# Normalising the attention probabilities on VectorE instead of GpSimd, in a two-layer cross-attention and RWKV kernel

## The reference

```python
attn = jnp.einsum('bkhd,bnhd->bhkn', q, kmat) / DH
attn = jnp.where(full_mask[:, None, None, :], attn, -jnp.inf)
attn = jax.nn.softmax(attn.astype(jnp.float32), axis=-1)      # the change is inside this line
attn_out = jnp.einsum('bhkn,bnhd->bkhd', attn, v) @ out_w + out_b + residual
out = gelu(rmsnorm(attn_out) @ mlp_w1 + mlp_b1) @ mlp_w2 + mlp_b2 + residual
# layer 1: layer norm, token shift, five mixed inputs (w, k, v, r, g), then per head
#   out_t = r_t (u k_t v_t + s);  s = k_t v_t + w_t s;  group norm, gate, Wo, layer norm, channel mixing
```

## Time and profile before

| | |
|---|---|
| time, median of 3 runs | 1182.81 us (1182.03 to 1183.99) |
| the profiled execution | 1185.69 us, of which the span of its instructions is 1183.9 us |
| mean granted TensorE clock | 0.935 of full speed |
| TensorE busy | 1031.7 us, 87% |
| VectorE busy | 814.1 us, 69% |
| ScalarE busy | 715.7 us, 60% |
| GpSimd busy | 467.4 us, 39% |
| the 128 normalisations (L956), on GpSimd | 134.7 us busy |

### The profile page before, as it was taken

One profiled execution on the slowest core, in us unless ns is written; L12 is line 12 of the kernel. 1 busy time (PEld: TensorE's weight loads), 2 busy tenths in 40 slices (PEclk: granted clock), 3 DMA queues, 4 the chain that ended last, 5 costly groups with the idle time before them and its releaser, 6 DMA issues.

```text
span 1183.9 us, 20422 instructions
## 1 busy us (share of the span) xinstructions
PE 1031.7 (87%) x6760; PEld 764.9 (65%) x6760; DVE 814.1 (69%) x1275; ACT 715.7 (60%) x2006; POOL 467.4 (39%) x391
## 2 busy tenths in 40 slices
PE   5878989898998989898998989999898999988744
PEld 3656667676766767666676767677676767666523
DVE  2347677686867688696767768686776868677562
ACT  4466574848666493956658394765749476674312
POOL 1124263453425354343535434342534524253240
PEclk9799989899998999999998989899898989989776
DMA  4405050321415041231505033151503215050310
GB/s 140 144 27 78 27 74 13 62 41 46 70 41 73 14 79 23 55 60 41 73 18 89 8 67 48 41 74 41 73 14 62 41 42 73 18 74 10 47 34 9
DMA packets 37127, 61.02 MB, mean 52 GB/s; under 512 B 10464, under 2 KB 13088, under 8 KB 36896
## 3 DMA queue, kind: packets, MB, share of 16 engines
q1 hardware_dynamic: 37024, 59.72, 27.9%
HBM read 21.95 MB, written 4.19 MB: 22 GB/s over the span
## 4 chain that ended last, share of the span: by engine, by line
PE 65%; ACT 14%; issue 7%; DVE 7%; POOL 5%; DMA 1%; SPq 0%; DVEq 0%; ACTq 0%; POOLq 0%
PE psum L366 31%; PE psum L467 9%; ACT probs L612 7%; PE psum L391 4%; POOL xm L964 3%; PE psum L538 3%; PE psum L384 3%; PE psum L371 2%; PE psum L415 2%; DVE xf L747 2%; PE psum L429 2%; PE psum L498 2%; PE psum L441 1%; ACT L582 1%; PE psum L485 1%
## 5 line engine op out<-in xcount | busy, mean ns | idle before, releaser
L981 POOL TENSOR_TENSOR rs<-st,rr 128x512 f32<-128x512 f32 x128 | 185.4, 1453 | 225.5 <-DVE st L911 202.9
L964 POOL TENSOR_TENSOR xm<-tmp,xs 128x512 f32<-128x512 f32 x80 | 92.8, 1176 | 299.3 <-DVE tmp L889 265.4
L911 DVE TENSOR_TENSOR_SCAN st<-decay,kv 128x512 f32<-128x512 f32 x128 | 202.0, 1588 | 1.5 <-POOL rs L981 1.3
L612 ACT ACTIVATE probs<-psum,neg_max 128x128 f32<-128x128 f32 x512 | 179.0, 385 | 1.6 <-DVE neg_max L795 1.3
L956 POOL TENSOR_TENSOR probs<-probs,rsum 128x512 f32<-128x512 f32 x128 | 134.7, 1057 | 86.8 <-DVE rsum L800 85.4
L366 PE MATMUL psum<-xm,w_sb 128*128 128x256 f32 x512 | 149.5, 444 | 7.6 <-POOL xm L964 5.7
L366 PEld LDWEIGHTS psum<-xm,w_sb 128*128 128x128 f32 x512 | 110.3, 224 | 33.2 <-POOL xm L964 11.9
L641 ACT ACTIVATE hid<-psum,vec 128x256 f32<-128x256 f32 x128 | 53.5, 470 | 123.7 <-PE psum L467 93.1
L366 PE MATMUL psum<-y,w_sb 128*128 128x256 f32 x512 | 117.7, 383 | 2.9 <-issue 1.8
L612 ACT ACTIVATION_READ_ACCUMULATOR probs<-psum,neg_max 128x1 f32 x512 | 115.8, 226 | 0.0
L467 PE MATMUL psum<-hid,w_sb 128*128 128x256 f32 x512 | 115.7, 379 | 0.0
(11 more groups left out here) (121 smaller groups left out, 1857.6 us busy)
## 6 DMA issues: line engine op xcount, KB each, us to landing
vb<-vr SPq DMA_DIRECT2D x128, 256.0 KB, 7.5
h_sb<-hT SPq DMA_DIRECT2D x16, 512.0 KB, 3.8
xa_sb<-xT SPq DMA_DIRECT2D x16, 256.0 KB, 4.0
out<-x SPq DMA_DIRECT2D x16, 256.0 KB, 2.0
mask_i<-maskT SPq DMA_DIRECT2D x16, 128.0 KB, 3.4
w_sb<-W SPq DMA_DIRECT2D x2, 768.0 KB, 6.8
w_sb<-W SPq DMA_DIRECT2D x1, 1280.0 KB, 7.1
w_sb<-W SPq DMA_DIRECT2D x1, 1248.0 KB, 9.1
```

Source lines behind the costliest of these rows:

```text
L612: last = fn(probs[:, u % PROBS, n, :], bank(g, f"s{u}")[:, n * P:(n + 1) * P], ACT.Exp, bias=neg_max[:, u % PROBS, n:n + 1], accum_out=sum ...
L911: nc.vector.tensor_tensor_scan(st[:, n % 2, :], decay[:, :, :, :].rearrange("p h b s -> p (h b s)"), kv[:, j, :, :].rearrange("p b s -> p ...
L964: tt(xm[:, k % XM, :, :].rearrange("p h (b s) -> p (h b) s", b=GB), tmp[:, k % TMP, :, :].rearrange("p h (b s) -> p (h b) s", b=GB), xs[0] ...
L981: tt(rs[:, (RH * g + n) % RS, :], st[:, n % 2, :], flat(rr), ALU.mult).then_inc(rs_made.sem, 1)
```

## The change

The eight `pn` pieces leave GpSimd's list and enter VectorE's, each directly behind the `in` piece of its unit. The code of the piece moves with them: it is the same multiplication of the same 128x512 operands, waiting for `rsum_made`, which is now an event of VectorE's own, and signalling `norm_made`, for which the transposes of TensorE wait. Nothing else is changed: buffers, the other orders and the transfers are as before.

```diff
@@ DVE_ORDER, POOL_ORDER @@
-DVE_ORDER = """2:hv0 3:gn 2:nm0 1:mx0 3:og 2:sx0 2:z 1:mx1 1:mx2 3:res 3:hm1 1:mx3 2:tm0 2:tm1 1:in0 2:tm2 1:in1 3:ct1 2:tm3 2:tm4 3:hv1 1:in2 1:mx4 1:mx5 1:in3
-1:pt0 1:mx6 3:nm1 1:mx7 1:in4 1:pt2 3:sx1 1:in5 3:xf0 1:in6 1:in7 1:pt4 1:pt6 2:kv0 1:at0 2:kv1 1:fold0 2:st0 1:at1 2:st1 1:y 3:xf1 1:ysum 2:kv2 2:kv3
+DVE_ORDER = """2:hv0 3:gn 2:nm0 1:mx0 3:og 2:sx0 2:z 1:mx1 1:mx2 3:res 3:hm1 1:mx3 2:tm0 2:tm1 1:in0 1:pn0 2:tm2 1:in1 1:pn1 3:ct1 2:tm3 2:tm4 3:hv1 1:in2 1:pn2
+1:mx4 1:mx5 1:in3 1:pn3 1:pt0 1:mx6 3:nm1 1:mx7 1:in4 1:pn4 1:pt2 3:sx1 1:in5 1:pn5 3:xf0 1:in6 1:pn6 1:in7 1:pn7 1:pt4 1:pt6 2:kv0 1:at0 2:kv1
...
-POOL_ORDER = """2:rs2 2:rs3 2:rs4 2:rs5 2:rs6 2:rs7 3:act 3:fin 1:xm0 1:xm1 1:xm2 0:pn0 0:pn1 1:xm3 0:pn2 0:pn3 1:xm4 0:pn4 0:pn5 0:pn6 0:pn7 1:rk 1:rs0 1:rs1"""
+POOL_ORDER = """2:rs2 2:rs3 2:rs4 2:rs5 2:rs6 2:rs7 3:act 3:fin 1:xm0 1:xm1 1:xm2 1:xm3 1:xm4 1:rk 1:rs0 1:rs1"""
@@ VectorE's pieces @@
+                elif piece[0:2] == "pn":
+                    u = int(piece[2:])
+                    wait(ve, rsum_made, g, u + 1)
+                    tt(probs[:, u % PROBS, :, :], probs[:, u % PROBS, :, :], rsum[:, u % PROBS, :].unsqueeze(2).broadcast_to([P, 4, KEYS]),
+                       ALU.mult).then_inc(norm_made.sem, 1)
@@ GpSimd's pieces @@
-                if piece[0:2] == "pn":
-                    u = int(piece[2:])
-                    wait(po, rsum_made, g, u + 1)
-                    tt(probs[:, u % PROBS, :, :], probs[:, u % PROBS, :, :], rsum[:, u % PROBS, :].unsqueeze(2).broadcast_to([P, 4, KEYS]),
-                       ALU.mult).then_inc(norm_made.sem, 1)
-                elif piece[0:2] == "xm":
+                if piece[0:2] == "xm":
```

More of the change, by code:

```diff
@@ L68 @@
 0:pt5 0:pt7 1:decay 0:ev1 0:ysq 2:relu"""
-DVE_ORDER = """2:hv0 3:gn 2:nm0 1:mx0 3:og 2:sx0 2:z 1:mx1 1:mx2 3:res 3:hm1 1:mx3 2:tm0 2:tm1 1:in0 2:tm2 1:in1 3:ct1 2:tm3 2:tm4 3:hv1 1:in2 1:mx4 1:mx5 1:in3
-1:pt0 1:mx6 3:nm1 1:mx7 1:in4 1:pt2 3:sx1 1:in5 3:xf0 1:in6 1:in7 1:pt4 1:pt6 2:kv0 1:at0 2:kv1 1:fold0 2:st0 1:at1 2:st1 1:y 3:xf1 1:ysum 2:kv2 2:kv3
-2:kv4 1:yn 2:st2 2:kv5 0:mask 2:st3 2:gate 2:bonus 2:st4 2:kv6 2:st5 1:fold1 2:kv7 2:st6 2:st7 1:x1 1:hm0 2:sum 1:ct0 3:fin 1:fold2"""
-POOL_ORDER = """2:rs2 2:rs3 2:rs4 2:rs5 2:rs6 2:rs7 3:act 3:fin 1:xm0 1:xm1 1:xm2 0:pn0 0:pn1 1:xm3 0:pn2 0:pn3 1:xm4 0:pn4 0:pn5 0:pn6 0:pn7 1:rk 1:rs0 1:rs1"""
+DVE_ORDER = """2:hv0 3:gn 2:nm0 1:mx0 3:og 2:sx0 2:z 1:mx1 1:mx2 3:res 3:hm1 1:mx3 2:tm0 2:tm1 1:in0 1:pn0 2:tm2 1:in1 1:pn1 3:ct1 2:tm3 2:tm4 3:hv1 1:in2 1:pn2
+1:mx4 1:mx5 1:in3 1:pn3 1:pt0 1:mx6 3:nm1 1:mx7 1:in4 1:pn4 1:pt2 3:sx1 1:in5 1:pn5 3:xf0 1:in6 1:pn6 1:in7 1:pn7 1:pt4 1:pt6 2:kv0 1:at0 2:kv1
+1:fold0 2:st0 1:at1 2:st1 1:y 3:xf1 1:ysum 2:kv2 2:kv3 2:kv4 1:yn 2:st2 2:kv5 0:mask 2:st3 2:gate 2:bonus 2:st4 2:kv6 2:st5 1:fold1 2:kv7 2:st6 2:st7
+1:x1 1:hm0 2:sum 1:ct0 3:fin 1:fold2"""
+POOL_ORDER = """2:rs2 2:rs3 2:rs4 2:rs5 2:rs6 2:rs7 3:act 3:fin 1:xm0 1:xm1 1:xm2 1:xm3 1:xm4 1:rk 1:rs0 1:rs1"""
 SP_ORDER = """0:mask 1:load0 0:h 1:xa 2:spread 0:row0 2:row1 1:s0 1:load1 3:store"""
```

## The result

The changed kernel takes 1204.99 us, median of four runs (1204.05 to 1207.44), against 1182.76 for the kernel before, measured beside it; the ratio is 1.0183 with a 95% interval of 1.0166 to 1.0199. It is slower by 22.2 us where 6 were forecast, and outside the stated range.

The account below looks back on a forecast made before the run. The prediction took a chain of waits through each group, plus TensorE's half clock, as the bound. Fifteen periods at +0.45 us (+6.8) and -0.3 for the first group gave a median of 1189 us, range 1177 to 1201.

Parts of the forecast that it names:

- the three xm: Sign on GpSimd: xm0 to xm2 would together take 3.85 us or more, against 3.45 before.
- the shorter wait of the transposes: Sign on TensorE: the last transposes would wait less than the 0.69 us they waited for GpSimd's pn6.
- sh1 would idle 0.5 us or more: Sign on ScalarE: sh1 would idle for VectorE's nm1, 0.5 us or more in each group.
- pn0 and pn1: Beside the mixed inputs xm0 to xm2: they would make V start 0.4 to 0.85 us later.
- the tie between pn1 and xm2: At xm1's end: V starts 0.4 us later if xm2 goes first, 0.85 if pn1 does.
- The length of a `pn`: Each multiplication on VectorE: 0.69 us, bounds 0.69 and 1.26, starting 0.10 us after its reciprocal.
- pn2 to pn7: pn2 and pn3 would delay nm1 and so sh1; pn6 and pn7 would end 0.3 us earlier before the last transposes.
- The sum at full clock: Net change of a group's period when TensorE keeps full clock: +0.75 to +1.2 us.
- of the second kind: Periods with half clock: +0.3 to +0.8 us, taken as 0.45, as V's later start brings some half clock back.
- the clock gives it back: Rival: a later V has less half clock until the period is unchanged; 1183 us, within 0.2%; chance 0.30.
- the shorter latency wins: Rival: xm0 to xm2 lose nothing, only 0.33 us gained at each group's end; -5.3, 1177.5 us; chance 0.20.
- The second stretch of half clock: Rival: the clock also falls between tr3 and va0; +12 beside the +6 if in half the groups, 1201 us; chance 0.08.

Follow-up runs that it names:

- e8_pn1_late: The changed kernel with only pn1 moved behind tm4, pn0 still directly behind its reciprocal; 1197.78 us, ratio 1.0126.
- e3_late: The changed kernel, all eight normalisations on VectorE, but with pn0 and pn1 moved behind tm4; 1187.06 us, ratio 1.0024.
- e10_after_td1: The changed kernel with one idle matmul call before xp0 and td1 computed three times over into the same bank; 1185.50 us, ratio 1.0013.
- e1_pool01: The changed kernel, but pn0 and pn1 stay on GpSimd, behind xm2; pn2 to pn7 are on VectorE; 1187.73 us, ratio 1.0032.
- e9_late_fill3: e7_late_fill with two more idle matmul calls before va0, into the bank of va0; 1177.39 us, ratio 0.9949.
- e7_late_fill: e3_late with one idle matmul call before xp0 and one before V in each group; 1184.32 us, ratio 1.0013.
- e12_before_wait: The kernel before with one more GpSimd step of 384 elements in front of xm1, into an unread scratch tensor; 1203.86 us, ratio 1.0182.
- e11_before_td1: The kernel before with one idle matmul call before xp0 and td1 computed twice; 1166.11 us, ratio 0.9849.
- e6_before_fill: The kernel before with one idle matmul call before xp0 and one before V in each group; 1167.52 us, ratio 0.9865.

## Why the prediction was right and wrong

- **The direction and the place** were right. V's start is what the change moves, and the exclusion between a VectorE step with two SBUF operands and GpSimd moves it: pn0 waited for xm0 and went before xm1, as the earlier trace rows had suggested. Of the signs named beforehand xm1 (1.6 us), the three xm (4.36) and the shorter wait of the transposes (12.8 us in all before, 3.2 after) came as said. That sh1 would idle 0.5 us or more in each group did not: it is 0.23 to 0.32.
- **pn0 and pn1** were put at 0.4 to 0.85 us, the tie between pn1 and xm2 left open. It fell to pn1 in every group, at 0.91. Each costs 0.45 (`e8_pn1_late`). The prediction's own times give 425.07 - 424.49 = 0.58 for the first, where it writes 0.4 to 0.5; what it writes is what came.
- **The length of a `pn`**, taken as 0.69 us, is 0.69 for most and 0.78 on average; longer are pn0 (0.97, beside xm0) and pn4 (about 1.2, beside xm4). Bounds of 0.69 to 1.26 held the mean. It starts 0.03 us after its reciprocal (495.43 to 495.46), not 0.10.
- **pn2 to pn7** were to cost 0.65 us at nm1 and give 0.3 back at the end, net 0.35. In `e3_late`, where pn0 and pn1 do no harm, it is 0.54 at sh1 and 0.25 back, net 0.3 (66.90 against 66.61). That is from groups at full clock, and in an order that has pn0 and pn1 before nm1 as well. In the changed kernel the two delays do not add: 0.91 and 0.3 would be 1.2, and the sum is 1.0.
- **The sum at full clock**, +0.75 to +1.2 per period, was right: +1.0 (two periods of `e10_after_td1`).
- **The step that failed** is the next one: "most are of the second kind, and I take 0.45, below its middle, because the clock is low at V's start there and each 0.1 us by which V is later brings some of it back". In place of +0.45 the period grew by 1.22. The clock gave nothing back: V at half clock takes 3.37 to 3.78 us, where it took 3.44 to 3.79. The half clock's share was 68.11 - 66.61 = 1.50 us per period before and is 69.33 - 67.6 = 1.7 after, on top of the whole 1.0 us; the 67.6 is that of `e10_after_td1`, as the changed kernel itself has no period of this kind. Fifteen times 1.22 is 18.3. The even periods at the end of the run before, from which I argued that a delay is absorbed, were one arrangement among several. The change made the gap before V longer and left no group at full clock there. Taking the full-clock value, 0.98, would have given +14.4, and the range would have needed the clock's extra beyond it.
- **The rivals.** That the clock gives it back (0.30) is refuted for the changed kernel, but `e1_pool01` behaves like it: sh1 comes a full us later there, and most periods are 68.2 us all the same, as in the kernel before. There V's wait is not longer; in the changed kernel it is. That the shorter latency wins (0.20) is too: even with pn0 and pn1 out of the way, `e3_late` is 1.0024. The second stretch of half clock, given 0.08, did not show as a cause in the changed kernel, but did in `e1_pool01`, and the fillers before va0 in `e9_late_fill3` took 7 us off `e7_late_fill`, more than was left of the loss against the kernel before without fillers.
- **Open:** why the same gaps bring the half clock in one group and not in the next. It is not haphazard: in `e12_before_wait` periods of 70.2, 69.1 and 68.9 us come round four times, in `e11_before_td1` 66.7, 66.7 and 67.9 three times. No run here was made to find what sets this. Executions of one kernel differ by some us too, and whether for the same reason is not shown: `e3_late` lay between 1183.8 and 1190.0, `e10_after_td1` between 1180.6 and 1186.4. The medians differ by 22.2 us where the profiled executions differ by 18.4, since that of before lies 2.9 us above its median and that of after 0.9 below. By the medians the loss is nearer to 1.5 us per period than to 1.22, and the rest of it stands in no trace.

## What to carry to other kernels

Before moving an elementwise step with two SBUF operands to VectorE, look at what GpSimd does at that moment. If GpSimd's step is on the path, the moved one is paid for there, whatever the loads of the engines; two steps moved to a place 3 us later gave back 18 of 22 us.

In this kernel a longer gap on TensorE cost its own length and kept the half clock coming besides. Take the work of a change at the period that has the full clock, and do not count on the half clock's share to shrink by as much: in `e1_pool01` the period stayed the same, in the changed kernel it did not. Try filling the gaps, with a bank that is free early enough, before anything else is reordered.

## What the runs showed of the hardware that was not expected

Useless matmuls made a tuned kernel faster: two calls per group, about 0.43 us each at full clock, gave 1.35% (`e6_before_fill`), and a second td1 with one call 1.5% (`e11_before_td1`). And 0.87 us more of idle TensorE in front of one projection cost 1.12 us per period, 69.23 against 68.11, with nothing changed but one GpSimd step (`e12_before_wait`). A waiting VectorE step with two SBUF operands went before GpSimd's next, queued one in each of the fifteen groups of the changed kernel.
